# Second layer: the attention's products ahead of the values', and a tile's sum and statistics in its own step

## The reference, cut to what matters

```python
q, k, v = relu(xn @ Wq.T + bq), relu(xn @ Wk.T + bk), xn @ Wv.T + bv      # 16 heads of 32
kv    = einsum('bnhd,bnhp->bhdp', k, v)
denom = maximum(einsum('bnhd,bhd->bnh', q, k.sum(axis=1)), 1e-6)
att   = einsum('bnhd,bhdp->bnhp', q, kv) / denom
y     = att + xn
attn  = (y - mean(y)) / sqrt(var(y) + 1e-5) * gamma + beta
xr, xk = mu_r * xn + (1 - mu_r) * xn_prev, mu_k * xn + (1 - mu_k) * xn_prev
ff    = sigmoid(xr @ W_r.T) * (square(relu(xk @ W_k.T)) @ W_v.T)
out   = x + attn + ff
```

## Time and profile before

| | us |
|---|---|
| median of 3 runs | 2221.1 (2219.8 to 2221.95) |
| the profiled execution's own time | 2221.37 |
| its span, first to last instruction | 2219.6 |
| start of the second layer's first matmul | 1435.64 |
| one group of the second layer (1858.27 to 1906.04) | 47.77 |

### The profile page before, as it was taken

How to read it: one execution, slowest core, us unless ns; L and a number is a source line. 1 busy time by engine, 2 the same in 40 slices (tenths; PEclk the granted TensorE clock), 3 DMA queues, 4 the chain that set the end, 5 groups by cost and what they waited for, 6 DMA issues and landing times. The chain is left out here.

```text
span 2219.6 us, 27604 instructions
## 1 busy us (share of the span) xinstructions
PE 2104.8 (95%) x9466; PEld 1669.8 (75%) x9466; DVE 1504.8 (68%) x2947; ACT 1057.2 (48%) x1769; POOL 824.4 (37%) x842
## 2 busy tenths in 40 slices
PE   7999999599769999999999999599999999999997
PEld 6888888344358888888888888478888888888886
DVE  5666554556467777777677775277777777777775
ACT  3445555323235555555455554264555444555442
POOL 1021000254345444444444443033443443443443
PEclk9999999799889999999999999799999999999999
DMA  4235333666523333332243331412222212221111
GB/s 146 100 124 167 119 124 119 227 197 199 197 88 102 114 119 100 114 123 96 95 152 123 97 112 67 142 39 90 82 96 67 67 67 86 86 95 67 67 39 39
DMA packets 173430, 241.40 MB, mean 109 GB/s; under 512 B 18793, under 2 KB 109161, under 8 KB 172138
## 3 DMA queue, kind: packets, MB, share of 16 engines
q1 hardware_dynamic: 161800, 216.63, 29.5%
q10 hardware_dynamic: 11490, 23.00, 2.8%
HBM read 138.86 MB, written 100.73 MB: 108 GB/s over the span
## 5 line engine op out<-in xcount | busy, mean ns | idle before, releaser
L99 PE MATMUL bank<-e_ring,e_w_hi 128*128 128x512 f32 x512 | 204.4, 399 | 22.8 <-DVE e_ring L1451 17.0
L1135 PE MATMUL bank<-d_kh,d_nat 128*128 128x512 f32 x768 | 196.0, 404 | 5.5 <-DVE d_kh L1031 5.5
L100 PE MATMUL bank<-e_ring,e_w_hi 128*128 128x512 f32 x512 | 200.6, 392 | 0.0
L101 PE MATMUL bank<-e_ring,e_w_lo 128*128 128x512 f32 x512 | 200.2, 391 | 0.0
L1451 DVE TENSOR_TENSOR e_ring<-e_mixed,e_ring 128x512 fp32r<-128x512 f32 x128 | 96.0, 750 | 122.7 <-ACT e_ring L1349 122.7
L1380 ACT ACTIVATE e_kr<-bank 128x512 f32<-128x512 f32 x64 | 38.0, 593 | 290.2 <-PE bank L101 232.4
L875 POOL TENSOR_TENSOR rstd<-d_var_eps,neg_half 128x1 f32<-128x1 f32 x64 | 35.1, 549 | 360.6 <-DVE d_var_eps L1051 360.6
L1135 PEld LDWEIGHTS bank<-d_kh,d_nat 128*128 128x128 f32 x768 | 141.3, 191 | 35.3 <-issue 6.5
L1326 POOL TENSOR_TENSOR e_x<-e_x,e_beta 128x512 f32<-128x512 f32 x64 | 82.8, 1293 | 223.8 <-ACT e_y L1371 223.8
L1332 POOL TENSOR_TENSOR e_x<-e_x,e_ff 128x512 f32<-128x512 f32 x64 | 82.4, 1288 | 207.4 <-DVE e_ff L1500 207.4
L99 PEld LDWEIGHTS bank<-e_ring,e_w_hi 128*128 128x128 f32 x512 | 96.7, 189 | 51.0 <-DVE e_ring L1451 19.2
(11 more groups left out here) (209 smaller groups left out, 6350.6 us busy)
## 6 DMA issues: line engine op xcount, KB each, us to landing
scr_v<-b_vt SPq DMA_DIRECT2D x64, 256.0 KB, 2.7
scr_z<-b_zt SPq DMA_DIRECT2D x64, 256.0 KB, 2.1
c_z<-scr_z SPq DMA_DIRECT2D x64, 256.0 KB, 2.8
scr_y<-c_y ACTq DMA_DIRECT2D x64, 256.0 KB, 2.8
d_x<-in_L_attn_x SPq DMA_DIRECT2D x64, 256.0 KB, 4.2
d_ut_raw<-scr_y SPq DMA_DIRECT2D x32, 512.0 KB, 4.1
d_v<-scr_v SPq DMA_DIRECT2D x32, 512.0 KB, 5.1
scr_x<-d_x SPq DMA_DIRECT2D x64, 256.0 KB, 2.1
```

Source lines behind the costliest of these rows:

```text
L99: eng.matmul(out, lhs[hi], rhs[hi], start=first, stop=False, skip_group_check=onto)
L100: eng.matmul(out, lhs[hi], rhs[lo], start=False, stop=False, skip_group_check=onto)
L101: return eng.matmul(out, lhs[lo], rhs[hi], start=False, stop=last, skip_group_check=onto)
L1135: mm = pe.matmul(BG[c][:, :], s[:, i, cols], r[:, j, :], start=M % NTB == 0 and i == j, stop=M % NTB == NTB - 1 and i == 1, skip_group_che ...
```

## The change

On TensorE, C(t) is issued before V(t). The wait for the queries (`q_done`) that this needs is added at the first tile. The waits of V(t) for its bank stay where they were, and so stand ahead of C(t).

On VectorE, the attention stands first in a tile's step, then `plain`, then the gated product, then the statistics of the same tile (before: of the tile before), then the output of the tile before (before: two tiles back). The loop has 5 steps, not 6.

On POOL, y + att comes first, then x + ff, then the root of the same tile.

The number of instructions, their sizes and their operands are the same.

```diff
@@ gpsimd
                 if t < GT:
                     n = g * GT + t
+                    pool.wait_ge(c_done, 2 * (n + 1))
+                    nc.gpsimd.tensor_tensor(y[t][:, :], y[t][:, :], att[t % 2][:, :], ALU.add).then_inc(sum_done, 1)
                     pool.wait_ge(ff_done, n + 1)
                     pool.wait_ge(shifted, n + 1)
                     nc.gpsimd.tensor_tensor(x2[h][:, t, :], x2[h][:, t, :], ff[t % 2][:, :], ALU.add)\
                       .then_inc(base_done, 1)
-                    pool.wait_ge(c_done, 2 * (n + 1))
-                    nc.gpsimd.tensor_tensor(y[t][:, :], y[t][:, :], att[t % 2][:, :], ALU.add).then_inc(sum_done, 1)
-                if t >= 1:
-                    n = g * GT + t - 1
                     pool.wait_ge(stat, 3 * n + 3)
-                    nc.gpsimd.tensor_tensor(rstd[(t - 1) % 2][:, :], var_eps[:, :], keep["neg_half"][:, 0:1],
-                                            ALU.pow).then_inc(rstd_done, 1)
+                    nc.gpsimd.tensor_tensor(rstd[t % 2][:, :], var_eps[:, :], keep["neg_half"][:, 0:1], ALU.pow)\
+                      .then_inc(rstd_done, 1)
@@ vector, body
-            for t in range(GT + 2):
+            for t in range(GT + 1):
                 if t < GT:
-                    tile_products(g, h, t)
-                if not last and t < GT:
-                    plain(g + 1, h, t)
-                if 1 <= t <= GT:
-                    tile_stats(g, t - 1)
-                if t >= 2:
-                    tile_out(g, h, t - 2)
+                    attention(g, t)
+                    if not last:
+                        plain(g + 1, h, t)
+                    gated(g, t)
+                    tile_stats(g, t)
+                if t >= 1:
+                    tile_out(g, h, t - 1)
@@ tensor, body
                     if g == 0:
                         pe.wait_ge(w_lo, LO + 4 * KT)
-                tokens_out(t, keys, wv).then_inc(v_full, 1)
+                if t == 0:
+                    pe.wait_ge(q_done, KT * (g + 1))
                 if n:
                     pe.wait_ge(c_done, 2 * n)
                 for a in range(KT):
...
                 mm.then_inc(c_full, 1)
+                tokens_out(t, keys, wv).then_inc(v_full, 1)
```

More of the change, by code:

```diff
@@ L1483, in body, with attention @@
                     mix(g + 1, 1 - h, 0, t, mu_k)
-            for t in range(GT + 2):
+            for t in range(GT + 1):
                 if t < GT:
-                    tile_products(g, h, t)
-                if not last and t < GT:
-                    plain(g + 1, h, t)
-                if 1 <= t <= GT:
-                    tile_stats(g, t - 1)
-                if t >= 2:
-                    tile_out(g, h, t - 2)
-        def tile_products(g, h, t):
-            n = g * GT + t
[L1496 to L1500, removed]
+                    attention(g, t)
[5 more added lines that the diff above has]
+                    tile_out(g, h, t - 1)
+        def attention(g, t):
+            n = g * GT + t
             dve.wait_ge(c_full, n + 1)
@@ L1519, in tile_products, with gated @@
                     rden[:, c, :, :].unsqueeze(3).broadcast_to([P, 2, HP, HD]), ALU.mult).then_inc(c_done, 1)
+        def gated(g, t):
+            n = g * GT + t
+            dve.wait_ge(v_full, n + 1)
+            dve.wait_ge(gate_done, n + 1)
+            if n >= 2:
+                dve.wait_ge(base_done, n - 1)
+            nc.vector.tensor_tensor(ff[t % 2][:, :], RVB[t % 2][:, :], gate[:, t, :], ALU.mult).then_inc(ff_done, 1)
         def tile_stats(g, t):
```

## The result

The changed kernel takes 2253.1 us (2252.7 to 2255.6) against 2220.5 beside it: 1.5% slower, ratio 1.0150, 95% interval 1.0132 to 1.0167. The prediction was 2262, in a range of 2242 to 2288.

What follows compares the result with a forecast made beforehand. TensorE was taken to bound the second layer. The profiled 2221.4 us plus 39.8 for fifteen groups and 0.4 for the tail gave 2261.6; 2262 was predicted, range 2242 to 2288.

Steps and rivals of the forecast that it cites:

- What bounds the stage: Second layer: TensorE bounds it, busy 47.47 of 47.77 us in a group, and each wait is paid 15 times.
- C held by the attention before it: TensorE waits at C(2) for att(1), 1.0 us, and at C(3) for att(2), 1.9 us, in each group.
- VectorE's chain: VectorE's tile steps up to att(2): start 1.96, 3.22 to statistics, 1.70 statistics, 0.66 output; att(2) ends at 13.78.
- The cost of a group: Second layer: each group 2.65 us longer (28.5 less 25.9 at Q(0)), 39.8 us over fifteen groups.
- The hand-over: From the end of POOL's sum to VectorE's statistics: 0.17 us allowed.
- The old wait at Q(0): TensorE's 0.46 us wait for VectorE's keys at Q(0) is swallowed, as TensorE's 28.5 ends after the key chain's 26.5.
- The tail: Last group, to the end: early attention gains nothing, as the same VectorE chain closes it; +0.4 us.
- The first rival: TensorE's clock falls after the stops at C, 1.4 us more a group, 2283 us; chance 0.26.
- POOL's sum: POOL's y + att, the deciding term: 1.66 us with `plain` beside it, against 1.28 alone.
- the second rival: POOL's sum is short, as VectorE's new order leaves POOL alone: 2246 us; chance 0.12.
- that collision: End of VectorE's statistics step: the scaling, with two SBUF inputs, could collide with POOL's x + ff; no size given.

Runs made afterwards that it cites:

- c_vfirst: The changed kernel with V(t) issued ahead of C(t) on TensorE again, VectorE and POOL as changed: 2249.8 us, ratio 1.0136.
- b_lag: The changed kernel with the lags of before (statistics one tile, output two), C still ahead of V: 2224.3 us, ratio 1.0018.
- e_twosets: The changed kernel with a second pair of banks for C, so C(t) waits for att(t-2): 2220.4 us, ratio 1.0003.
- f_lag_twosets: The changed kernel with both edits, those of b_lag and of e_twosets: 2223.8 us, ratio 1.0016.
- g_root_twosets: f_lag_twosets with POOL's root of the tile before put ahead of x + ff: 2209.0 us, ratio 0.9951.

## Why the prediction was right

**What bounds the stage.** Right. TensorE does, and what it lost in a group was paid in each: 2.2 us a group, and 0.8 more in the first, gave the 33.9 between the first and the last.

**C held by the attention before it.** Right, in place and nearly in size: waits at C(2) and C(3) and at no other C in a steady group, and c_vfirst, b_lag and e_twosets each moved as this says, b_lag by 6 us less. C(2) comes 0.93 late and C(3) another 1.80, where I had 1.0 and 1.9. As idle time the profile shows 0.76 and 1.56, 36.6 us in all; I had said 40 to 45, mostly by taking the delay for the idle time. Group 0 also has a wait at C(1), and 0.8 us more in all; I had counted it like the others.

**VectorE's chain.** The mechanism was right and one term too large. I allowed 0.17 from POOL's end to the statistics; the rows show 0.03 (1877.55 + 1.65 to 1879.23). The step from an attention to its statistics is 3.08, not 3.22, and twice 0.14 brings C(3) to 13.62, where I had 13.9. The start at 1.96, the sum at 1.66, the statistics step at 1.70 and the output at 0.66 came out as taken. VectorE's wait was 0.5 to 0.6 in a step and not 0.8, by that 0.14 and by my leaving out small pieces between the instructions.

**The cost of a group.** 2.65 predicted, 2.23 measured. The hand-over is most of it: Q(0) comes 28.24 after C(0), not 28.5. The rest is that I compared Q(0) with Q(0): before, Q(0) was itself a restart after a wait, and from it to the next V(0) took 21.90, where it now takes 21.76. I had counted the restarts only on the new side. The profiled execution's own time is 2252.7 where my sum gave 2261.6. Of these 8.9 us the groups are 5.9 (39.8 predicted, 33.9 measured), the earlier start of the second layer 3.2 and the tail 0.6, less the 0.8 that group 0 took longer to its V and C part. So the 3.2 us by which this execution started early are luck in the number and no part of the reasoning.

**The old wait at Q(0).** Right: swallowed. VectorE reaches the key part 23.70 after C(0), where I had 24.3 and before it was 23.72. Four times the 0.14 make that 0.6.

**The tail.** I said +0.4; it is -0.2. The last group's step from an attention to its statistics is 2.69, not 2.84, three times over, and that is most of the 0.6.

**The clock.** The first rival did not come: the clock is 1.00 over a group with idle times of 0.76 and 1.56, and over the whole stretch from 1500 to 2190 us. 1.56 is the size of the stop that kept its clock in the earlier trace rows, and below the 1.99 of the two that lost it. My chain was 0.14 a step too long, so I had put the second wait nearer to the bad side than it is. No run says what a stop between 1.56 and 1.99 would have done, so on this point the rows gave a chance and no reason.

**POOL's sum.** 1.65 with `plain` beside it, so the second rival did not come either. The rule of the Trainium skill that I weighed there (GPSIMD Engine Reference, Key points: contention with VectorE instructions of two SBUF inputs) is the one on which the later runs turned, and the traces agree with it (1.43 and 0.99 beside x + ff, 0.75 without). In the changed kernel itself the scaling starts so late in x + ff (1.09 after its start) that it still takes 0.75.

I had named that collision as possible and put no number on it, though the trace of before has one. Another VectorE piece with two inputs in SBUF takes 1.27 there, beside POOL's x + beta, and 0.75 alone:

```profile
1897.70 1.27 DVE L1444 SCALAR_TENSOR_TENSOR e_mixed<-e_xt,cols,e_prev 128x512 f32<-128x512 f32 x1 [0.83 <-ACT e_prev L1358]
```

```profile
1897.13 1.29 POOL L1326 TENSOR_TENSOR e_x<-e_x,e_beta 128x512 f32<-128x512 f32 x1 [0.81 <-ACT e_y L1371]
```

It ends 0.55 after POOL's end. This row could have warned of the 6 and 12 us by which b_lag and f_lag_twosets missed the theory.

## What to carry to other kernels

Before a product is issued earlier, ask who empties its banks and what stands ahead of that in the emptying engine's queue: an earlier issue brings the deadline forward by its whole distance (2.7 us here), for every buffer behind it. A lag of one step between a sum on one engine and its use on another is cheap and hides a hand-over; taking it out put 1.7 us of statistics and 0.6 of waiting ahead of the next read. And where two engines slow each other, choose the order on both, so that the one with time to spare pays: the same work on POOL in another order made 14.8 us.

## What the runs showed of the hardware that I had not expected

A VectorE `scalar_tensor_tensor` with two SBUF inputs, 0.75 us alone, that starts while POOL's 128x512 `tensor_tensor` runs ended 0.55 us after POOL's end in each of the cases shown, wherever it had started (0.41, 0.57, 0.85 and 0.85 after POOL's start): 1.43, 1.27, 0.99 and 0.99 us. It holds far beyond these: in the ten traces of this case, from 1500 us on, more than 1000 VectorE instructions with two SBUF inputs start while such a POOL instruction runs, and each that has a row of its own ends 0.52 to 0.58 after it, `tensor_tensor` ones too. It looks as if VectorE's instruction had mostly to wait POOL's out; what is done in the 0.55 was not looked into. A VectorE instruction with one input in SBUF is not stretched: the gated product, whose other input is a bank, starts 0.48 after y + att and takes its 0.69 (1878.03, above).

The other way round POOL's own is stretched: y + att takes 1.65 beside a `plain` that started 0.17 before it, and 1.28 in the last group, without it. In these traces the one that starts second pays. POOL's root, 128x1, did not stretch the scaling beside it (0.74, in g_root_twosets), though it takes 1.0 us itself.

TensorE kept 2.4 GHz (granted clock 1.00) through two stops a group, 0.76 and 1.56 us of idle time, in 14 groups one after the other. How much longer a stop would cost it the clock is open.
